# A graph network kernel: the interaction stage's basis products go to three PSUM banks in a new order, and the node result is read one step sooner

## What is computed

```
p1    = tanh(p @ pp_W1 + pp_b1) @ pp_W2 + pp_b2
inter = concat(p1[idx_i], p1[idx_j]) @ pi_W1 + pi_b1      # [edges, 128] -> 64
inter = (inter @ pi_W2 + pi_b2) @ pi_W3                   # [edges, 64 * 8]
i1    = einsum('ecb,eb->ec', inter.reshape(E, 64, 8), basis)
i1    = tanh(i1 @ ii_W1 + ii_b1) @ ii_W2 + ii_b2
out   = segment_sum(i1, idx_j)
```

## Time and profile before

| | us |
|---|---|
| median of three runs (lowest, highest) | 10138.35 (10131.53, 10139.61) |
| the profiled execution's own time | 10130.24 |
| its span in the profile | 10128.6 |
| PE busy | 5756.1 |
| DVE busy | 4352.4 |
| ACT busy | 2451.7 |
| POOL busy | 6779.5 |

### The profile page before, as it was taken

The page is one execution under the profiler, slowest core; times in us unless marked ns, Lnnn a source line. Parts: engine busy times, 40 slices in busy tenths (PEclk is TensorE's granted clock), DMA queues, the critical chain, the costliest instruction groups (busy, mean ns, idle before and its releaser), DMA issues.

```text
span 10128.6 us, 209066 instructions
## 1 busy us (share of the span) xinstructions
PE 5756.1 (57%) x32026; PEld 3578.1 (35%) x32026; DVE 4352.4 (43%) x12092; ACT 2451.7 (24%) x4667; POOL 6779.5 (67%) x7783
## 2 busy tenths in 40 slices
PE   6999998244444447999999972444444422222222
PEld 4777774122222223444444432333333211121111
DVE  6888886232323235777777761111111111111111
ACT  5999995000000002333333320000000000000000
POOL 3333331777777775777777757777777677777777
PEclk9999999555555558999999985555555555555555
DMA  3333333111111112222222221111111111111111
GB/s 109 96 96 97 96 97 131 27 31 30 31 30 30 30 31 50 61 62 61 61 61 60 61 42 28 29 28 29 29 29 29 26 28 29 29 29 29 29 29 28
DMA packets 563973, 489.90 MB, mean 48 GB/s; under 512 B 307755, under 2 KB 361840, under 8 KB 563824
## 3 DMA queue, kind: packets, MB, share of 16 engines
q0 software_dynamic: 215488, 230.46, 12.7%
q1 hardware_dynamic: 315952, 255.93, 8.9%
q10 hardware_dynamic: 32448, 2.65, 0.2%
HBM read 427.12 MB, written 62.00 MB: 48 GB/s over the span
## 4 chain that ended last, share of the span: by engine, by line
POOL 35%; PE 32%; issue 16%; DVE 7%; ACTq 5%; DMA 3%; ACT 1%; POOLq 1%; DVEq 1%; SPq 0%
POOL mov L741 33%; PE ps L1695 6%; PE ps L1520 5%; PE ps L1546 4%; ACTq L392 4%; PE ps L1553 3%; PE ps L1687 3%; POOL outs L741 2%; PE ps L1714 1%; DVE scr L1011 1%; PE ps L1680 1%; PE ps L1676 1%; PE ps L1544 1%; DMA mov<-tab_msg,idx 1%; PE ps L1705 1%
## 5 line engine op out<-in xcount | busy, mean ns | idle before, releaser
L1520 PE MATMUL ps<-outs,mov 128*64 128x64 f32 x9984 | 1371.1, 319 | 3882.6 <-DMA mov<-tab_q,idx 1429.5
L1520 PEld LDWEIGHTS ps<-outs,mov 128*64 128x64 f32 x9984 | 1158.4, 221 | 4204.3 <-issue 4202.9
L911 DVE TENSOR_TENSOR acc<-acc,ps 64x64 f32 (+1 forms) x1664 | 352.8, 212 | 4259.2 <-PE ps L1520 4085.9
L741 POOL DMA_INDIRECT outs<-tab_u,idx x1664 | 1583.9, 952 | 580.6 <-issue 479.1
L741 POOL DMA_INDIRECT mov<-tab_h,idx x1612 | 1528.7, 948 | 559.6 <-issue 469.6
L741 POOL DMA_INDIRECT mov<-tab_msg,idx x1612 | 1538.1, 954 | 518.2 <-issue 463.2
L741 POOL DMA_INDIRECT mov<-tab_q,idx x1612 | 1527.0, 947 | 528.1 <-issue 490.9
L1011 DVE TENSOR_TENSOR scr<-ps,scr 128x512 f32<-128x512 f32 x1664 | 1063.9, 686 | 361.4 <-PE ps L1687 334.2
L1695 PE MATMUL ps<-scr,w_bas 128*64 128x512 f32 x3328 | 898.6, 618 | 0.0
L705 POOL TENSOR_TENSOR scr<-outs 128x128 f32<-128x128 f32 x416 | 191.7, 461 | 814.0 <-DVE outs L921 813.2
L921 DVE TENSOR_TENSOR outs<-rel,iota_w 128x256 f32<-128x256 f32 x1664 | 706.2, 425 | 42.4 <-issue 29.0
(11 more groups left out here) (230 smaller groups left out, 8440.4 us busy)
## 6 DMA issues: line engine op xcount, KB each, us to landing
mov<-in_dst_row SPq DMA_DIRECT2D x832, 128.0 KB, 2.7
mov<-in_ea_T SPq DMA_DIRECT2D x416, 128.0 KB, 2.5
mov<-tab_msg SPq DMA_DIRECT2D x3328, 0.2 KB
mov<-tab_msg ACTq DMA_DIRECT2D x3328, 0.2 KB
mov<-tab_h SPq DMA_DIRECT2D x3328, 0.2 KB
mov<-tab_h ACTq DMA_DIRECT2D x3328, 0.2 KB
mov<-tab_q SPq DMA_DIRECT2D x3328, 0.2 KB
mov<-tab_q ACTq DMA_DIRECT2D x3328, 0.2 KB
```

The lines of the kernel that those rows point to most:

```text
L741: nc.gpsimd.indirect_dma_start(out=gat(e, u)[:, k, :], out_offset=None, in_=table, in_offset=bass.IndirectOffsetOnAxis(ap=idx[:, u, k:k + ...
L911: nc.vector.tensor_tensor(into, into, bank(banks[u % len(banks)])[0:rows, 0:W], ALU.add) \
L1520: last = mm(bank(banks[u % len(banks)])[0:width, 0:W], values(u)[:, k, :], sel(e, u)[:, k, :], start=k == 0, stop=k == TL - 1)
```

## The change

The spread products go to banks 2, 3 and 7 in turn (`SPREAD`), and `SPREAD_BACK` says how many z's before its own z the last reader of that bank is. S2 and S5 are the ones in bank 7. PE's order becomes: inter, S2 S3 S4, W0 W1, S5 S6, W2 W3, transposes, S7, W4 W5, S0, W6 W7, S1, sum. Since `result2` writes into bank 7 too, PE now waits after it for the first `ordered` count of DVE's `result`, and DVE's `result` stands at step 1 instead of 2.

```diff
+SPREAD = (2, 3, 7, 2, 3, 7, 2, 3)
+SPREAD_BACK = (2, 2, 5, 3, 3, 3, 3, 3)
...
-                        nc.vector.tensor_tensor(zed[:, b % SL, :], bank(2 + b % 2), inter[:, u % 2, b % 2, :], ALU.mult) \
+                        nc.vector.tensor_tensor(zed[:, b % SL, :], bank(SPREAD[b]), inter[:, u % 2, b % 2, :], ALU.mult) \
...
-                return [(2, result), (3, norm3)]
+                return [(1, result), (3, norm3)]
...
-                        pe.wait_ge(z_done, done2_of(NBAS, g, it, u, b, 2))
-                        mm(bank(2 + b % 2), pair[:, b, :], bas[:, u, :], start=True, stop=True).then_inc(bas_spread, 1)
+                        pe.wait_ge(z_done, done2_of(NBAS, g, it, u, b, SPREAD_BACK[b]))
+                        mm(bank(SPREAD[b]), pair[:, b, :], bas[:, u, :], start=True, stop=True).then_inc(bas_spread, 1)
...
                     last.then_inc(sum_of.sems["formed"], 1)
+                    wait_flow(pe, sum_of, "ordered", turn0, g)
+                    pe.sem_inc(pe_turn, 1)
...
                 chunk_loop(pe, [
-                    (3, inter_stage), (4, spread(2)), (4, spread(3)), (4, weigh(0)), (4, weigh(1)),
-                    (4, spread(4)), (4, spread(5)), (4, weigh(2)), (4, weigh(3)), (5, turn_tan),
-                    (4, spread(6)), (4, spread(7)), (4, weigh(4)), (4, weigh(5)),
-                    (3, spread(0)), (3, spread(1)), (4, weigh(6)), (4, weigh(7)), (6, sum_pair)], per=2,
+                    (3, inter_stage), (4, spread(2)), (4, spread(3)), (4, spread(4)), (4, weigh(0)), (4, weigh(1)),
+                    (4, spread(5)), (4, spread(6)), (4, weigh(2)), (4, weigh(3)), (5, turn_tan),
+                    (4, spread(7)), (4, weigh(4)), (4, weigh(5)), (3, spread(0)),
+                    (4, weigh(6)), (4, weigh(7)), (3, spread(1)), (6, sum_pair)], per=2,
                            nodes=(WAIT_TURNS + 2, [(1, result2)]))
```

## The result

The changed kernel takes 10177.56 us (median of six, 10174.68 to 10178.41) against 10137.53 (six, 10131.53 to 10143.35) for the kernel before: 40.0 us more, a ratio of 1.0039 with a 95% interval of 1.0027 to 1.005. It is slower, as forecast, and inside the range; the forecast of +61 us was half as large again as the change. The profiled executions, 10174.68 and 10130.24, lie 44.4 apart. 38.8 of that is the stretch of the stage's gathers: 6009.1 - 3859.6 = 2149.5 us after, 2110.7 before. The other 5.6 lie outside that stretch and were not followed further.

The account below looks back on a forecast made before the run. PE was taken to bound the 45 turns with node work; -0.60 + 1.05 + 0.8 + 0.10 = +1.35 us per turn, +61 us in all, gave 10198 us, range 10160 to 10235.

Parts of the forecast that it names:

- What bounds the stage: Interaction stage: POOL paces turns 0 to 6, PE turns 7 to 51; POOL's floor is 40.2 us per turn.
- Step 3: Turn's step with DVE's norm: third bank buys one S ahead, end at 11.43 instead of 12.03 us, -0.60.
- Rival 1: Third bank absorbs DVE's norm, so PE runs on: -0.47 us per turn, 10117 us; faster in all 7%.
- PE's own work: An undisturbed PE step: bf16 followed by f32 once more, +0.10 us, 9.52 for 9.42; bounds 0 and 0.2.
- Step 2: Step that DVE's node result leaves: PE had no gap to give back, so +0.10 us.
- The hold: End of step 0: PE waits for DVE's node result before inter, 1.31 us, bounds 0.9 and 1.6.
- rival 2: The hold is half covered, 0.9 us, and step 1 costs +0.3: +0.24 per turn, 10149 us; 9%.
- Step 0: Step with PE's node product: waiting -0.36, own work +0.10, new hold 1.31; net +1.05 us.
- The rest of waiting: In step 0, 0.36 us of PE's waiting beside the node product's 0.40; forecast to go wholly.
- Step 1: Step that DVE's node result enters: late z's delay S5, S6 and W2/W3, +0.8 us, bounds 0.3 and 1.2.
- the 18 us that I put on my row: Boundary charge of 0.4 us per turn over 45 turns, from a first-stage trace row, instead of the skill's drain rule.

Follow-up runs that it names:

- e8: Changed kernel with the node product in bank 6 and PE's wait for DVE's result removed, measured again: 10173.7 us, ratio 1.004 to the kernel before.
- l3: The kernel of e7 with three of four gathers of the interaction stage left out, run once: 10065.89 us.
- e1: Changed kernel with the node product in bank 6 and PE's wait for DVE's result removed: 15861.08 us, ratio 1.0103 to the kernel before.
- e6: The changed kernel unedited, beside the kernel before: 15686.53 against 15463.13 us, ratio 1.0151.
- e5: Changed kernel, node product in bank 6, no PE wait, DVE's result between step 1's sel and adds: 15750.52 us, ratio 1.0045 to the kernel before.
- l1: The kernel before with three of four gathers of the interaction stage left out, run once: 10101.06 us.
- l4: The kernel before with S1 moved directly ahead of the sum and three of four gathers left out, run once: 10094.40 us.
- e7: The kernel of e5 measured again, beside a kernel before of 10131.58 us: 10105.0 us, ratio 0.9972.

## Why the prediction was right, and where its size was off

- **What bounds the stage: right.** PE's turn from turn 7 on; 45 times the turn's loss is 38.7 of the 40.0 us.
- **Step 3, -0.60: right in mechanism,** -0.61. S2 goes at once (5412.78 is 1.75 behind inter), the gap in front of S4 moves to S5 and stays at 0.87. z0, started when the norm ends, is what PE needs; a third bank buys one S ahead. Rival 1 falls with it. The exact size is luck: W2 starts at 6.12 against the forecast 5.96, and what stands behind it takes 5.27 against 5.47. Both come from PE's own work, the last point below. Step 2 ends 0.21 sooner than forecast while DVE's norm takes as long as ever (4.94 from z7 to z0), so inter comes earlier and z0 0.16 later behind it, at 1.59.
- **The hold, 1.31: right in size, half right in cause.** 5433.68 - 5431.99 = 1.69 instead of 0.40, so 1.29. In it, too, two errors cancel: from the node product's start to the result's end it was 5432.98 + 0.34 - 5431.99 = 1.33, not 1.51 (the two DVE instructions overlap, as rival 2 said), and from there to inter 0.36, not 0.2. e8 shows that it is not a price of its own: take it away and step 1 pays as much.
- **Step 0, net +1.05: +1.09, by two errors that cancel.** The rest of waiting didn't vanish: 11.26 - 9.31 - 0.40 - 1.29 = 0.26 is still there (S6 waits for z3), and l3 has more of it. I had DVE's z0 start 2.72 behind z7; over the loop's turn it was 5422.18 - (5418.34 + 0.74) = 3.10. PE's own work, on the other hand, was less than I took.
- **Step 1, +0.8: mis-sized, +0.49.** W2 starts 5438.35 - 5433.68 = 4.67 behind inter, not 4.84: since PE was let go 0.16 later behind the result than forecast, z0 was that much less late. The rest is PE's own work.
- **PE's own work, +0.10 a step: the wrong sign, -0.11,** and outside its bounds of 0 and 0.2. This is the step that failed. In an unheld step it is the whole difference between 9.52 and 9.31, and it accounts for 0.21 in step 2 and 0.21 in step 1, of the 0.49 by which the turn was missed. S1 ahead of the sum costs 5421.54 - 5421.31 = 0.23, what S to S costs, not 0.31, and the sum then takes 0.89. I had priced the place by the earlier trace rows. But the product there uses 3 rows of the array (3*128) and what follows 128: rows of the array change, not only the format. So the 0.31 in the earlier trace rows is no evidence for a cost of bf16 before f32. The same row had a second sign: its eight f32 products take 1.16, as the sum does directly behind W in the earlier trace rows, where behind S1 the sum's eight take 1.05. From the starts, it is the first of the eight alone: 0.21 to the second one behind W and behind the 3-row product, 0.11 behind S1.

By the Trainium skill, TensorEngine Tiling (Array Packing), Key Properties, a change of tiling mode drains the engine. I had set that aside, and the traces agree with it: 0.31 into W (half-width), 0.23 where S and sum are both full. The 0.31 in the earlier trace rows fits as well, if a product of 3 rows counts as a mode of its own, which no run tested. Without the 18 us that I put on my row instead, the forecast would have been 10180, but its nearness to 10177.56 is partly luck: by the rule, as I counted it, PE's own work stays as it was. Here the number of changes stayed at eight a step and the time still fell by 0.11, so what stands behind a change matters too: behind W the sum of 128-column products takes 0.99, and 0.89 with a 512-column spread in between, which itself costs no more than its usual 0.23.

## What to carry over

When an engine's side task is moved, ask first what the engine was doing in the place it leaves and the place it enters: here 1.9 us per turn hung on two instructions of DVE that take 0.6 us together, as they were placed ahead of the multiplications that another engine needed and behind a product that came last, and taking out the visible wait only moved it. A forecast whose parts come out right can still owe that to errors that cancel; compare the parts of the parts, as above for step 3 and the hold. Put such a task where its input is long there and its successor isn't next. Before a price is taken from a row elsewhere in the trace, compare all of its shape, rows of the array included.

## What was not expected of the hardware

Beside e1 to e6 the kernel before took 1.5 times as long, and so did the changed kernel in e6. Its first stage, in which PE is the busiest, ran as ever (499 of 500 us from 500 to 1000 in both traces); from the second stage on, where POOL's gathers begin, everything was slower. SP's issues in e6 (start, duration): six in a row as ever, 0.62 to 0.72 us apart, and in the next half turn 2.1 to 4.9 us apart.

```profile
7060.66 0.51 SPq L610 DMA_DIRECT2D mov<-in_dst_row  x1
7061.38 0.47 SPq L613 DMA_DIRECT2D win<-tab_v  x1
7062.03 0.41 SPq L615 DMA_DIRECT2D bas<-basis_parts  x1
...
7079.65 0.69 SPq L610 DMA_DIRECT2D mov<-in_dst_row  x1
7082.46 0.71 SPq L613 DMA_DIRECT2D win<-tab_v  x1
7087.36 0.70 SPq L615 DMA_DIRECT2D bas<-basis_parts  x1
```

Between them stand single register instructions of SP, many of them 0.7 us long: in e6 3205 of SP's 27124 took over 0.5 us, the first at 1780 us, in the first trace of the changed kernel none took even 0.3. DVE meanwhile stood still for up to 12 us. I read this as a starved supply of instructions, which is not shown; what starved it was not tested. It is no property of one chip: e1 to e5 ran on chip 0 and e6 on chip 7, and l1 to l4, later on the same chip 7, and the kernel before beside them (10129.58) were free of it, as were e7 and e8 on chip 4. It ruled over the edits: the version that wins by 0.28% loses by 0.43% there, and the changed kernel's loss grew from 0.39 to 1.51%. Why some steps of a turn stall and others don't stays open.
